# Another order of maxima, roundings, root steps and A's low half in a kernel of gated cross attention and routed low-rank experts

## The reference

```python
def xattn(q, k, v, ...):                     # q = layernorm(x), k = v = ctx
    qh = einsum('bcn,oc->bon', q, Wq)        # 8 heads of 64, o = 512
    kh = einsum('bcn,oc->bon', k, Wk)
    vh = einsum('bcn,oc->bon', v, Wv)
    qh = softmax(qh, over the 64 of a head) * 64 ** -0.5
    kh = softmax(kh, over n)
    context = einsum('bhdn,bhen->bhde', kh, vh)
    out = einsum('bhde,bhdn->bhen', context, qh)
    out = einsum('bcn,oc->bon', out, Wo) + bo
    return out / sqrt(sum(out * out, over channels)) * g * sqrt(128)
x = x + tanh(g_xattn) * xattn(layernorm(x), ctx, ctx)

def ffn(x, A, B, Wr):                        # 2048 rows of 1024, 64 experts of rank 16
    scores = x @ Wr.T
    gates = softmax of the 16 largest of 64 scores, 0 elsewhere
    h = einsum('nd,krd->nkr', x, A) * gates
    return einsum('nkr,kdr->nd', h, B) * 2
x = x + tanh(g_ffn) * ffn(layernorm(x))
```

## Time and profile before

| | before |
|---|---|
| median of 3 runs | 942.69 us (940.84 to 943.14) |
| profiled execution | 941.5 us |
| its span | 939.5 us |
| mean granted clock of TensorE | 0.989 |
| busy: TensorE | 902.3 us |
| busy: VectorE, ScalarE, GpSimd | 740.4, 687.1, 515.6 us |

### The profile page before, as it was taken

The page is one execution under the profiler, slowest core; times in us unless marked ns, Lnnn a source line. Parts: engine busy times, 40 slices in busy tenths (PEclk is TensorE's granted clock), DMA queues, the critical chain, the costliest instruction groups (busy, mean ns, idle before and its releaser), DMA issues.

```text
span 939.5 us, 15942 instructions
## 1 busy us (share of the span) xinstructions
PE 902.3 (96%) x4732; PEld 765.1 (81%) x4732; DVE 740.4 (79%) x1517; ACT 687.1 (73%) x1408; POOL 515.6 (55%) x340
## 2 busy tenths in 40 slices
PE   7899999999999999999989998599999999999997
PEld 5687888887787888788878787599999999999886
DVE  6888889988898898889877768687777777777631
ACT  4787797778768777876776747678888888888732
POOL 3786678788878978887787944222222222222100
PEclk9999999999999999999999999799999999999999
DMA  4324433453544335333412883111121111111001
GB/s 156 115 88 139 156 113 119 152 181 104 166 159 145 115 131 174 100 124 112 160 50 83 270 304 119 57 68 68 68 68 68 68 68 67 67 67 67 23 23 46
DMA packets 35175, 104.04 MB, mean 111 GB/s; under 512 B 4416, under 2 KB 11584, under 8 KB 35136
## 3 DMA queue, kind: packets, MB, share of 16 engines
q1 hardware_dynamic: 29376, 82.59, 25.3%
q0 software_dynamic: 5472, 20.45, 6.9%
q10 hardware_dynamic: 288, 0.52, 0.2%
HBM read 79.43 MB, written 24.12 MB: 110 GB/s over the span
## 4 chain that ended last, share of the span: by engine, by line
PE 66%; POOL 9%; DVE 8%; issue 8%; ACT 7%; DMA 1%; POOLq 0%; ACTq 0%; SPq 0%; DVEq 0%
PE ps L61 20%; PE ps L63 19%; PE ps L62 19%; PE ps L1437 4%; PE ps L1446 3%; POOL qe L447 3%; ACT qe L679 2%; POOL ctx_lo L406 2%; ACT h_raw L772 1%; PE ps L1427 1%; POOL qhalf L440 1%; ACT qT_hi L687 1%; POOL aT_lo L460 1%; POOL xn_lo L426 1%; ACT y_raw L772 1%
## 5 line engine op out<-in xcount | busy, mean ns | idle before, releaser
L518 POOL TENSOR_TENSOR rb<-u_in,rb 128x1024 f32<-128x1024 f32 x14 | 33.7, 2405 | 233.8 <-DVE rb L990 233.8
L447 POOL TENSOR_TENSOR qe<-qe,qrec 128x1024 f32<-128x1024 f32 x64 | 121.2, 1903 | 15.0 <-DVE qrec L1008 15.0
L61 PE MATMUL ps<-aT_hi,yT_hi 128*128 128x448 f32 (+2 forms) x360 | 119.8, 333 | 0.9 <-DVE yT_lo L1143 0.9
L772 ACT ACTIVATE h_raw<-hg 32x256 f32<-32x256 f32 x256 | 106.3, 415 | 17.7 <-DVE hg L1157 14.9
L62 PE MATMUL ps<-aT_hi,yT_lo 128*128 128x448 f32 (+2 forms) x360 | 118.6, 329 | 0.0
L63 PE MATMUL ps<-aT_lo,yT_hi 128*128 128x448 f32 (+2 forms) x360 | 118.4, 329 | 0.0
L440 POOL TENSOR_TENSOR qhalf<-qe 128x512 f32<-128x512 f32 x64 | 82.2, 1284 | 63.5 <-ACT qe L679 61.6
L1014 DVE TENSOR_TENSOR qT_lo<-ps,qT_hi 128x512 fp32r<-128x512 f32 x128 | 81.5, 678 | 34.8 <-ACT qT_hi L687 34.3
L61 PE MATMUL ps<-bT_hi,hT_hi 128*128 128x512 f32 x240 | 94.5, 394 | 2.7 <-DVE bT_lo L1049 2.3
L772 ACT ACTIVATE y_raw<-u_in 32x256 f32<-32x256 f32 x224 | 92.8, 414 | 3.3 <-DVE u_in L1148 0.8
L62 PE MATMUL ps<-bT_hi,hT_lo 128*128 128x512 f32 x240 | 94.2, 393 | 0.0
(11 more groups left out here) (178 smaller groups left out, 2559.6 us busy)
## 6 DMA issues: line engine op xcount, KB each, us to landing
x_in<-in_x SPq DMA_DIRECT2D x16, 512.0 KB, 3.3
ctx_in<-in_ctx SPq DMA_DIRECT2D x16, 512.0 KB, 5.5
ctxT_in<-in_ctxT SPq DMA_DIRECT2D x16, 512.0 KB, 3.3
ctxT_hi<-in_ctxT POOLq DMA_DIRECT2D x16, 512.0 KB, 4.1
u_scratch<-osb SPq DMA_DIRECT2D x16, 512.0 KB, 3.0
out<-res SPq DMA_DIRECT2D x16, 512.0 KB, 2.8
x<-in_x SPq DMA_DIRECT2D x15, 512.0 KB, 3.9
turn_scratch<-ek SPq DMA_DIRECT2D x14, 512.0 KB, 4.4
```

Of the source, the lines that this page charges most:

```text
L61: nc.tensor.matmul(psum, whi, mhi, start=start, stop=False)
L447: nc.gpsimd.tensor_tensor(v, v, w, ALU.mult).then_inc(q_norm, 1)
L772: last = nc.scalar.activation(dst[32 * q:32 * q + 32, 256 * a:256 * a + 256], src[32 * a:32 * a + 32, 256 * q:256 * q + 256], ACT.Copy)
```

## The change

Inside an element of stage one (elements 1 to 14 unless said otherwise):
- GpSimd: `lo_moved_k` goes from behind m's low half to behind `normalise(b, 0)` and `hi_c(b)`, ahead of `lo_ctx(b+1, 0)`. `lo_a` goes from behind m's low half to the head of the next element. `early_newton` goes from the middle of element 14 to its end.
- VectorE: `lo_q(b-1, 1)` goes ahead of `scale_m`; the maximum of q1 ahead of that of k2; the last seven root steps go from ahead of `scale_m` to behind the two maxima, ahead of `sum_q(b, 0)`.
- ScalarE: the rounding of q1 goes ahead of the exponential of k1; the rounding of the moved k goes from ahead of the rounding of q2 to behind the exponential of q1.
- TensorE: the second shift goes ahead of the first half of the output.

In element 15 the two spreads of the norms come later on VectorE. In call 16 the transposes, rounding and low half of y(0) come ahead of those of q1, and `up(0, 0)` ahead of the transposes of q2; the statistics of y come earlier; each strip of A has a counter of its own.

At the boundary strips 2 to 7 of B's low half are GpSimd's (four of them were); VectorE makes strips 0 and 1 ahead of the row sum; the sums of the third output are taken ahead of the last gating, and three routing steps of b=1 before the loop. In `ffn_body` 1 and 2 TensorE takes the column sums one piece later, and `result(0)`, `part_u(4)` and `lo_moved_h(1)` are done at the end of b=1. At the end, VectorE moves half of the last h, and the last output leaves in two halves.

The diff, cut to what the text speaks of:

```diff
-    return k in (2, 3, 5, 7)
+    return k >= 2
...
-    for b in (NB - 2, NB - 1):
-        sp.wait_ge(res_done, 2 * b + 2)
-        sp.dma_start(out[b], res[b % 2][:, :]).then_inc(out_stored[b % 2], 16)
+    sp.wait_ge(res_done, 2 * NB - 2)
+    sp.dma_start(out[NB - 2], res[0][:, :]).then_inc(out_stored[0], 16)
+    for h in range(2):
+        v = slice(512 * h, 512 * h + 512)
+        sp.wait_ge(res_done, 2 * NB - 1 + h)
+        sp.dma_start(out[NB - 1][:, v], res[1][:, v]).then_inc(out_stored[1], 16)
     for half in range(2):
-        sp.wait_ge(out_stored[half], 16 * (NB // 2))
+        sp.wait_ge(out_stored[half], 16 * (NB // 2 + half))
...
-        nc.gpsimd.dma_start(aT[0][:, t, :], AT[t]).then_inc(a_ready, 16)
+        nc.gpsimd.dma_start(aT[0][:, t, :], AT[t]).then_inc(a_ready[t], 16)
...
-    def body(b, head, tail, ahead, split=False):
-        if split:
+    def body(b, head, tail, ahead, low=False, cast=False):
+        if low:
+            lo_a(b - SPLIT - 1)
+        if cast:
             cast_a(b - SPLIT)
         if tail:
             halve(b - 1, 3)
@@ -538,17 +544,13 @@
             pool.wait_ge(m_hi, b)
             nc.gpsimd.tensor_tensor(mts[1][:, :, :], mt[:, :, :], mts[0][:, :, :].bitcast(f32),
                                     ALU.subtract).then_inc(m_lo, 1)
-        if split:
-            lo_a(b - SPLIT)
-        if head and turned(b):
-            lo_moved_k(b)
-        if isinstance(b, int) and b == NB - 2:
-            early_newton()
         if head and not ahead:
             add_first(0)
         if head:
             normalise(b, 0)
             hi_c(b)
+            if turned(b):
+                lo_moved_k(b)
...
         if head:
             halve(b, 2)
+        if isinstance(b, int) and b == NB - 2:
+            early_newton()
...
     pool.sem_inc(a_low, 1)
-    with pool.Fori(SPLIT, SPLIT + DC) as b:
-        body(b, head=True, tail=True, ahead=True, split=True)
-    with pool.Fori(SPLIT + DC, NB - 2) as b:
-        body(b, head=True, tail=True, ahead=True)
+    body(SPLIT, head=True, tail=True, ahead=True, cast=True)
+    with pool.Fori(SPLIT + 1, SPLIT + DC) as b:
+        body(b, head=True, tail=True, ahead=True, low=True, cast=True)
+    body(SPLIT + DC, head=True, tail=True, ahead=True, low=True)
...
-    def move_groups(dst, src, s):
-
-        for a in range(P // 32):
+    def move_groups(dst, src, s, groups=range(P // 32)):
+
+        for a in groups:
...
-        move_groups(h_raw, hg, h_moved)
+        move_groups(h_raw, hg, h_moved, range(2 if isinstance(b, int) and b == NB - 1 else P // 32))
...
         if tail and not head:
+            hi_y(0)
             hi_q(b - 1, 1)
-            hi_y(0)
-            hi_q(b - 1, 2)
...
             exp_q(b, 0)
+            if tail:
+                hi_q(b - 1, 1)
             exp_k(b, 1)
         if tail:
-            if head:
-                hi_q(b - 1, 1)
             hi_m(b - 1)
             if not head:
+                hi_q(b - 1, 2)
...
         if head and turned(b):
-            hi_moved_k(b)
             hi_q(b - 1, 2)
         elif head:
             hi_k(b, 0)
         if head:
             exp_k(b, 2)
             exp_q(b, 1)
+        if head and turned(b):
+            hi_moved_k(b)
         if tail and head and not turned(b):
             hi_q(b - 1, 2)
...
+    hi_b(0)
+    hi_b(1)
     square_u(EARLY, 1, 1)
-    hi_b(0)
...
         hi_moved_h(b - 1)
-        if first:
-            hi_b(1)
...
+    def move_last_h():
+        dve.wait_ge(h_turned, NB)
+        for a in (2, 3):
+            for q in range(P // 32):
+                last = nc.vector.tensor_copy(h_raw[32 * q:32 * q + 32, 256 * a:256 * a + 256],
+                                             hg[32 * a:32 * a + 32, 256 * q:256 * q + 256])
+        last.then_inc(h_moved, 1)
...
@@ -1212,9 +1223,6 @@
             sum_q(b - 1, 2)
         if head and turned(b):
             turn_k(b)
-        if last:
-            dve.wait_ge(ctx_lo, 2 * NB)
-            spread(0, rb_first[0], n_newton, 4 * NEWTON)
         if ahead and started(b):
             stats(b + 1)
         if norms:
@@ -1231,33 +1239,34 @@
             max_q(b, 0)
             max_k(b, 1)
         if last:
-            dve.wait_ge(xn_lo, 2 * NB)
-            spread(1, rb_first[1], n_newton, 4 * NEWTON)
+            dve.wait_ge(ctx_lo, 2 * NB)
+            spread(0, rb_first[0], n_newton, 4 * NEWTON)
+        if tail and not head:
+            lo_y(0)
+            lo_q(b - 1, 1)
+        if tail and head:
+            lo_q(b - 1, 1)
+        if tail:
+            scale_m(b - 1)
+        if tail and not head:
+            stats2(1, 1)
+            lo_q(b - 1, 2)
+        if head:
+            max_q(b, 1)
+            max_k(b, 2)
+        if head and not turned(b):
+            lo_k(b, 0)
         if ahead and started(b):
             std(b + 1, range(3, NCH + 1))
-        if tail and not head:
-            lo_q(b - 1, 1)
-            lo_y(0)
-        if tail:
-            scale_m(b - 1)
-        if tail and head:
-            lo_q(b - 1, 1)
-        if tail and not head:
-            lo_q(b - 1, 2)
-            stats2(1, 1)
-        if head and turned(b):
-            max_k(b, 2)
-            max_q(b, 1)
-        elif head:
-            max_q(b, 1)
-            max_k(b, 2)
-            lo_k(b, 0)
         if not started(b):
             std(b + 1, range(5, NCH + 1))
         if head:
             sum_q(b, 0)
         if tail and head:
             lo_q(b - 1, 2)
+        if last:
+            dve.wait_ge(xn_lo, 2 * NB)
+            spread(1, rb_first[1], n_newton, 4 * NEWTON)
         if head:
             max_k(b, 3)
             max_q(b, 2)
...
@@ -1317,11 +1326,15 @@
     gated(0, 0)
     gated(0, 1)
     lo_y(1)
+    stats2_sums(2, 2)
     gated(0, 2)
     turn_h(0)
+    lo_b(0)
+    lo_b(1)
     part_u(EARLY)
-    stats2(2, 2)
-    lo_b(0)
+    std2(2, range(NCH + 1))
+    for n in range(3):
+        route_step(1, n)
...
+        second = isinstance(i, int) and b == 2
         if first:
             lo_moved_h(0)
-            lo_b(1)
-            for n in range(3):
-                route_step(1, n)
             turn_y(2, 0)
-            lo_b(4)
             for n in range(3, TOP):
                 route_step(1, n)
-            lo_b(6)
+        elif second:
+            turn_y(3, 1)
+            route(2)
+            norm_u(4)
         else:
             result(b - 2, (j + 1) % 2, (j + 3) % SLOTS, 2 * i + (j - 1) // 2)
             lo_moved_h(b - 1)
@@ -1355,7 +1368,10 @@
         if ahead:
             lo_moved_y(b + 1)
         if first:
-            norm_u(b + 2)
+            norm_u(3)
+            result(0, 0, 0, 0)
+            part_u(4)
+            lo_moved_h(1)
         if norms:
...
+    move_last_h()
     lo_moved_h(NB - 1)
...
-            pe.wait_ge(a_ready, 16 * DC)
...
         for m in range(DC):
+            if p == 0 and not started(b):
+                pe.wait_ge(a_ready[m], 16)
...
@@ -1562,11 +1580,11 @@
         if not head:
             context(b - 1, 0)
             context(b - 1, 1)
+            tr_y(0, 0)
             tr_q(b - 1, 1, next(turn))
-            tr_y(0, 0)
             fold(b - 1)
+            up(0, 0)
             tr_q(b - 1, 2, next(turn))
-            up(0, 0)
             output(b - 1, 0, range(CH))
             tr_q(b - 1, 3, next(turn))
             up(0, 1)
...
+        if head and turned(b):
+            shift_q(b, 1)
         if tail and head:
             output(b - 1, 0, range(CH // 2))
-        if head:
+        if head and not turned(b):
             shift_q(b, 1)
...
+        late = isinstance(i, int) and b <= 2
         up(b, 0)
-        if norms:
+        if norms and not late:
             sum_u(b + 2)
         up(b, 1)
+        if norms and late:
+            sum_u(b + 2)
         up(b, 2)
         down(b - 1)
```

More of the change, by code:

```diff
@@ L211, in flamingo_layer @@
         u_stored = sem("u_stored")
-        a_cast, a_low, a_ready = sem("a_cast"), sem("a_low"), sem("a_ready")
+        a_cast, a_low = sem("a_cast"), sem("a_low")
+        a_ready = [sem(f"a_ready{t}") for t in range(DC)]
         b_low_dve, b_low_pool = sem("b_low_dve"), sem("b_low_pool")
@@ L796, in hi_moved_h @@
                     act.wait_ge(f_mm, 2 * b)
-                act.wait_ge(h_moved, b + 1)
+                act.wait_ge(h_moved, NB + 1 if last else b + 1)
                 nc.scalar.activation(by_group((hT_last if last else hT)[0]), by_strip(h_raw),
@@ L895, in _ @@
             body(NB, head=False, tail=True, ahead=False)
+            hi_b(0)
+            hi_b(1)
             square_u(EARLY, 1, 1)
-            hi_b(0)
             def ffn_body(i, j):
                 b = SLOTS * i + j + 1
-                first = isinstance(i, int) and b == 1
-                if first:
+                if isinstance(i, int) and b == 1:
                     move_h(0)
                 hi_moved_h(b - 1)
-                if first:
-                    hi_b(1)
```

## The result

Before and after were timed side by side on one chip, four runs each: 941.77 us before (940.37 to 943.14) and 951.17 us after (951.0 to 952.79). The ratio is 1.0104, with a 95% interval of 1.0083 to 1.0125: slower by 9.4 us, where 7.4 us and a time of 950 us were forecast. The times lie closer than the losses only because the kernel before took 941.77 us here and 942.69 us where the forecast started from it. The profiled execution of after takes 951.3 us with a span of 949.6 us, against 939.5 us.

What follows compares the result with a forecast made beforehand. TensorE, busy 96% of the span, was taken as the bound; 15.8 - 3.0 + 2.0 - 0.9 - 5.0 - 1.5 = +7.4 us on the profiled 941.5 gave 948.9, or 950 us against the median; range 938 to 963.

Steps and rivals of the forecast that it cites:

- A: Stage one, elements 1 to 13: the moved k delays the context's low half, period 33.56 us, +15.8 us.
- The formula: Stage one: period = 32.5 + (start of the context's low half behind the shift - 13.74), not below 32.1 us.
- Rival 1: Stage one: the moved k stays hidden and the boundary decides, faster, 929 us; chance 0.13.
- Rival 2: Stage one: TensorE's new waits lower its clock, 1.3 us an element, +17, 967 us; chance 0.13.
- Rival 3: Whole kernel: gains and losses cancel with A at its lower bound, +4.6 us, giving 939 us; chance 0.12.
- Moves costed at nothing: Inside stage one's elements: the other moves, such as the second shift ahead of the first half output, cost nothing.
- B: Element 14: root steps go to its end, so it takes 33.56 us instead of 36.55, -3.0 us.
- C: Element 15: late root steps delay its shift some 1.2 us, the second spread counts 0.8; +2.0 us.
- D: Call 16: y(0)'s transposes and low half go ahead of q1, removing a 0.9 us wait; -0.9 us.
- E: Boundary to stage two: the 10.6 us row sum wait goes, two waits near 3 us come; -5.0 us.
- the ring: Stage two: ScalarE and VectorE's loop between h low halves takes 23.06 us, so TensorE must wait once it outruns it.
- F: The end: VectorE moves half the last h, TensorE's 1.05 us wait goes, output leaves in halves; -1.5 us.

Runs made afterwards that it cites:

- e3: The kernel before, with only the moved k's rounding and low half put where the change puts them: 947.26 us, ratio 1.0062.
- e6: The changed kernel, with the low half of A's strip put back ahead of the first q normalisation in 8 elements: 952.08 us, ratio 1.0101 to the kernel before.
- e2: The changed kernel, with only VectorE's last seven root steps put back ahead of the q1 low half and the scaling: 935.36 us, ratio 0.9941 to the kernel before.
- e1: The changed kernel, with only the moved k's rounding and low half put back in elements 1 to 14: 929.21 us, ratio 0.9879 to the kernel before.
- e7: The kernel before with the change's A strip, element 14 root steps, element 15 spreads, call 16, boundary, first two stage-two elements and end: 928.58 us, ratio 0.9845.
- e5: e1 with TensorE's column sums one piece later in every element of stage two, not only the first two: 923.17 us, ratio 0.9794 to the kernel before.
- e8: e7 with TensorE's column sums one piece later in every element of stage two: 921.65 us, ratio 0.9777 to the kernel before.

## Why the prediction was right, point by point

**A, the moved k and the late q sum: right in mechanism, too small by 3.6 us.** The formula held where TensorE waits for the low half: 15.02 us gives 33.8, and 33.79 was measured. It held in e3 too, and in e6. In e2 another wait comes to the same time, and in e1 and e7 the exp of k lifts some periods above the formula's lowest value. The first anchor of the formula was in part luck: of the eight elements with a strip in the kernel before, three (b=6, 7, 8) show their wait behind the exp of k and not behind the low half, with periods of 32.52 to 32.67 all the same. The start was forecast at 14.78. The missing 0.24 us lies in one term of VectorE's sum: I let the last k maximum take 1.1 us, the distance at which two reductions follow each other, but what stands behind it is a root step on a tiny tile, which starts 1.25 us behind it (290.68 to 291.93); the rest is the q maximum, 0.08 us late. Over the eight elements with a strip that made 10.0 us and not 8.3. The five plain ones made 9.4 and not 7.5, since the first three take 34.2 us, as they took 0.3 us more before. The forecast of 1.8 us of waiting an element was right as a delay (1.75 us by the starts), but the waits view, which counts idle time up to a modelled end, shows 1.19 us of it; so its sum is 17.6 us and not 14 x 1.8.

**Rival 1 (the moved k stays hidden)** needed a start of the low half by 13.3 us; it was 15.0. **Rival 2 (the clock)** falls: the granted clock is 1.00 over both waits of b=8 and over 47 to 522 us. Its price of 1.3 us was a remainder, and low. Behind the low half's wait in b=14, the same stretch of TensorE's program (from that product's second piece to the third matmul of the product with m) takes 3.71 us before (488.07 to 491.78) and 2.14 us in after (505.14 to 507.28): the lower clock costs 1.6 us. **Rival 3, A at its lower bound,** was not what happened, but e2 and e3 have its numbers: normalisation at 9.1 us, start 13.9, period 32.7, all three as that bound had them. Its reason, though, was the root steps' place and not a surplus of VectorE.

**Moves costed at nothing.** The strip of A is free in its new place and was free in its old one as well, once the q sum was late (e6). The second shift shows no wait of its own in b=8 of after, but in e2 it does (0.28 us). One gain I had not listed: at its old place, ahead of ScalarE's q work, the moved k's rounding waits for its transfer, and TensorE with it (0.29 to 0.48 us in b=6 to 8 of the kernel before, 0.44 in e1). At its new place that wait is gone, in after and in e2.

**B and C.** GpSimd's twelve root steps (513.0 to 518.2, 5.2 us) make the shift of b=15 wait 1.13 us, forecast 1.2, and the two landmarks are 1.8 us nearer, forecast 1.8.

**D** came as a wait that goes, and not as time: no wait for y(0) is left (0.88 us before, at 541.34), but C and D together give +0.2 against -0.1. A wait of 0.49 us for a q maximum has come in b=15 (537.87); the rest I did not trace.

**E, the boundary: -4.9 against -5.0.** TensorE got the row sum of b=3 at 639.18, which is 622.3 on the clock of the earlier trace rows (the moving of h(0) is 16.87 us later in after); forecast 622.1, and 628.87 before. That is 6.6 us, of which 1.7 went again: from that sum to the next it is 24.74 us and not 23.06. Waits of 3.75 and 4.56 us stood where I had put 3 and 3, and the stretch at half clock came. That was all priced in, but I took the second wait as the ring's price. It was not: e5 and e8 took it away but for 0.4 us, with the half clock behind it, for 6 to 7 us, and the sums stayed 23.06 us apart. What held TensorE there was the order of its own queue, where the sum stood one piece too early.

**F: -1.9 against -1.5.** TensorE's 1.05 us wait near the end is gone. That GpSimd's six strips of B delay nothing was right too: the last ended at 596.85, and TensorE's waits have no row for it.

## What to carry to other kernels

Cost moves along the chain that ends in the wait, and not one by one: the chain here had 1.5 us of room (11.8 to 13.3 us). The root steps alone stayed inside it, the moved k alone overran it by 0.6 us an element, and both together by 1.7, and taking one back gave 16 or 22 us. When a formula hits, look which wait the trace names: in e2 the number fitted and another path had come level. A gap ahead of a late step is no free place for the step behind it; put movable work in front of the wait, where e6 shows it costs nothing, and never between the late result and the engine that needs it. When one wait is left after a mend, try its place in the waiting engine's own queue before calling it the price of the others' speed.

## What the runs showed of the hardware

A subtraction of 128x1024 on VectorE took 3.38 us beside one of GpSimd's. In after, two such run before GpSimd starts its own at 581.32, and take 1.16 us each. In the kernel before, the two strips that VectorE makes behind the end of GpSimd's (575.51) take 1.18 and 1.22 us, and one beside them 2.31. From after:

```profile
579.47 2.32 DVE L1052 TENSOR_TENSOR bT_lo<-b_raw,bT_hi 128x1024 fp32r<-128x1024 f32 x2
```

So two strips together cost less than the one of 3.38 us had. And two idle stretches of TensorE, 0.91 and 0.28 us, 1.2 us apart, left its clock at 1.00 in b=8, while 3.75 and 4.56 us were followed by stretches of 0.70 and 0.74.
